# Attention scores: four 32-row groups of a batch issued together instead of two

## The reference, cut to what matters

```
x = x + attention(layernorm(x), ctx, ctx)          # layers 0 and 1
q, k, v = query @ Wq.T + bq, key @ Wk.T + bk, value @ Wv.T + bv    # 16 heads of 16
scores = einsum('bhsd,bhtd->bhst', q, k) / 4        # 128 x 128 for each batch and head
probs  = softmax(scores)                            # layer 1 adds a padding mask to the scores first
out    = einsum('bhst,bhtd->bhsd', probs, v) @ Wo.T + bo
```

## Time and profile before

| | |
|---|---|
| median of three runs | 1118.36 us |
| the profiled execution | 1119.13 us, its span 1117.3 us |
| PE busy | 952.8 us, 85% of the span |
| DVE busy | 776.6 us, 70% |
| ACT busy | 581.0 us, 52% |
| attention of layer 0 | about 49 to 232 us of the span |
| attention of layer 1 | about 600 to 768 us |
| score matmuls (L1343) | 512 records, 74.7 us of busy time in all |
| mean granted TensorE clock | 0.94 |

### The profile page before, as it was taken

The page is one execution under the profiler, slowest core; times in us unless marked ns, Lnnn a source line. Parts: engine busy times, 40 slices in busy tenths (PEclk is TensorE's granted clock), DMA queues, the critical chain, the costliest instruction groups (busy, mean ns, idle before and its releaser), DMA issues.

```text
span 1117.3 us, 20415 instructions
## 1 busy us (share of the span) xinstructions
PE 952.8 (85%) x6981; PEld 825.7 (74%) x6981; DVE 776.6 (70%) x1538; ACT 581.0 (52%) x1112; POOL 436.6 (39%) x479
## 2 busy tenths in 40 slices
PE   2798878748987999999837888885989999999995
PEld 2577667536877999999825767665678888888885
DVE  5688787866664777777655687795686666667665
ACT  5375675745234667667546877874622232322221
POOL 1465556240663666666415444334012212212210
PEclk9989999859998999999956899996899999999999
DMA  3300750010325888888540000001000001000002
GB/s 129 110 21 1 189 144 1 1 61 1 128 82 193 237 231 233 227 221 233 119 134 1 20 20 1 1 2 43 15 15 29 28 14 28 17 26 28 14 0 76
DMA packets 44281, 85.81 MB, mean 77 GB/s; under 512 B 4161, under 2 KB 31041, under 8 KB 44097
## 3 DMA queue, kind: packets, MB, share of 16 engines
q0 software_dynamic: 14784, 46.44, 15.1%
q1 hardware_dynamic: 29440, 38.61, 11.9%
HBM read 64.25 MB, written 20.79 MB: 76 GB/s over the span
## 4 chain that ended last, share of the span: by engine, by line
PE 48%; DVE 20%; ACT 11%; issue 9%; DMA 7%; POOL 4%; DVEq 0%; ACTq 0%; POOLq 0%
PE bank L1179 31%; PE bank L1215 8%; DMA w_raw<-in_fw,w_idx 4%; DVE nmax L1034 3%; PE bank L1274 3%; DVE probT_lo L1063 2%; PE bank L1364 2%; DVE prob L1037 2%; POOL sorted_x L375 2%; ACT xn L512 2%; DMA summed<-y_sb,tile_to 2%; ACT probT_hi L654 1%; ACT o_raw L644 1%; PE bank L1343 1%; ACT w_hi L533 1%
## 5 line engine op out<-in xcount | busy, mean ns | idle before, releaser
L1179 PE MATMUL bank<-xT_hi,w_hi 128*128 128x512 f32 x352 | 139.9, 398 | 2.2 <-DVE hid L964 2.2
L581 ACT ACTIVATE act_sb<-bank 128x512 f32<-128x512 f32 x88 | 52.6, 598 | 167.8 <-PE bank L1179 167.7
L1179 PE MATMUL bank<-xT_lo,w_hi 128*128 128x512 f32 x352 | 139.3, 396 | 0.0
L1179 PE MATMUL bank<-xT_hi,w_lo 128*128 128x512 f32 x352 | 139.1, 395 | 0.0
L964 DVE TENSOR_TENSOR hid<-bank,act_sb 128x512 f32<-128x512 f32 x88 | 60.8, 691 | 107.3 <-ACT act_sb L581 107.1
L332 POOL TENSOR_TENSOR w_hi<-w_raw,zero_col 128x768 fp32r<-128x768 f32 (+1 forms) x20 | 31.9, 1595 | 262.9 <-PE bank L1215 236.8
L951 DVE SCALAR_TENSOR_TENSOR xres<-bank,gate,xres 128x256 f32<-128x256 f32 x320 | 132.6, 476 | 0.8 <-PE bank L1215 0.8
L1364 PE MATMUL bank<-ident,prob 128*128 128x128 f32 x512 | 86.2, 298 | 31.9 <-DVE probT_lo L1063 26.0
L1063 DVE TENSOR_TENSOR probT_lo<-bank,probT_hi 128x512 f16<-128x512 f32 x128 | 88.0, 687 | 32.4 <-ACT probT_hi L654 31.8
L1179 PE MATMUL bank<-xsT_hi,w_hi 128*128 128x256 f32 x368 | 106.5, 289 | 2.3 <-DVE xsT_lo L918 1.5
L1215 PE MATMUL bank<-w_hi,hid_hi 128*128 128x256 f32 x352 | 99.5, 283 | 6.2 <-DVE hid_lo L972 6.2
(11 more groups left out here) (199 smaller groups left out, 2763.5 us busy)
## 6 DMA issues: line engine op xcount, KB each, us to landing
w_raw<-in_fw SPq DMA_DIRECT2D x18, 384.0 KB, 3.0
sorted_x<-empty_row SPq DMA_DIRECT2D x2, 2967.0 KB, 21.4
xs<-sorted_x SPq DMA_DIRECT2D x23, 258.0 KB, 3.4
ctx_raw<-in_ctxT SPq DMA_DIRECT2D x8, 512.0 KB, 5.2
aw_raw<-in_aw SPq DMA_DIRECT2D x10, 256.0 KB, 3.8
summed<-empty_row SPq DMA_DIRECT2D x1, 2304.0 KB, 29.6
xres<-in_x SPq DMA_DIRECT2D x4, 512.0 KB, 5.7
xn_all<-summed SPq DMA_DIRECT2D x4, 512.0 KB, 5.9
```

Source lines behind the costliest of these rows:

```text
L581: nc.scalar.activation(act_sb[:, (ls * J + j) % 2, :], bank[2 * ((ls * J + j) % 2) + 1][:], ACT.Silu).then_inc(f["act"], 1)
L1179: last = nc.tensor.matmul(dst, lh, rh, start=(i == 0), stop=(i == len(pairs) - 1))
```

## The change

`scores` now issues all four groups of a batch in one call, the first half of each of the four strips, in layer 1 then their masks, then the second half. It is called at steps 0, 4 and 8 rather than at every even step from 0 to 10, and once rather than twice ahead of the next block. Ahead of a batch it waits for both `sub` and for all four exponentials of the batch before. The number of matmuls is the same.

```diff
-                    b, g = divmod(i, NG)
+                    b = i // NG
...
                     if b >= 1:
-                        pe.wait_ge(a["sub"], n * 8 + (i - NG) // 2 + 1)
-                        pe.wait_ge(a["exp"], n * GROUPS + (i + 1 - NG + 1))
+                        pe.wait_ge(a["sub"], n * 8 + 2 * b)
+                        pe.wait_ge(a["exp"], n * GROUPS + i)
...
                     for u in range(KT):
-                        for r in (g, g + 1):
+                        for r in range(NG):
...
-                            for r in (g, g + 1):
+                            for r in range(NG):
...
                         if i + NG < GROUPS:
-                            if i % 2 == 0:
+                            if i % NG == 0:
                                 scores(n, i + NG)
...
                     if build:
-                        for g in range(0, NG, 2):
-                            scores(n + 1, g)
+                        scores(n + 1, 0)
...
-                for g in range(0, NG, 2):
-                    scores(0, g)
+                scores(0, 0)
```

## The result

The changed kernel takes 1174.51 us in the median (1172.32 to 1175.47, four runs), the kernel before beside it 1119.69 (four runs). The ratio is 1.048, with a 95% interval of 1.0449 to 1.0512: slower by 54.8 us, where 1172 had been predicted. The profiled execution of the changed kernel took 1175.47 us, with a span of 1173.6, which is 56.3 more than the span before.

A forecast was written before the change was run, and what follows sets the result against it. Though PE is busiest at 85%, a ring of ACT and DVE was taken to bound the edited steps. Waits of 37.9 us plus a clock term of 15.1 make 53.0 on 1119.13: 1172 us, range 1140 to 1194.

The forecast's parts named there:

- The saved calls count nothing: Score calls on PE: 29.8 us of work saved, counted at nothing because scores come 1.66 us early.
- the ring: Attention steps: ACT and DVE links E, O, H, L, M, sub, without PE; 3.66 us for two groups.
- The rival at 1089 us: Whole kernel: PE is the bound and the saved calls come back as time, 29.8 us; chance 0.06.
- The wait of 1.40, 1.44 and 1.62 us: Layer 0, steps 0, 4, 8: calls wait for the fourth exponential; 4.46 us a block, 37.9 us over both layers.
- The clock: Steps 4 and 8, three blocks per layer: PE's idle time halves its clock; 1.15 or 1.36 us each, 15.1 us.
- The clock's cost in the first blocks: First block of each layer: no clock cost counted, since the clock is at half there already.
- their terms: Last block of each layer, wait plus two slow calls: 6.76 us in layer 0, 7.7 us in layer 1.
- the column's sum: Predicted extra time of all eight blocks: each block's wait, plus two slow calls in all but the first blocks.
- That the time stays: Attention steps: engines emptying PSUM bound them, so saving and new wait both hide; 1119 us; chance 0.05.
- The waits without the clock: Attention: the waits cost 37.9 us and the clock holds, 1157 us; chance 0.27.
- The last rival: Attention: clock stays low through most, 1195 us, or strips don't run side by side, over 1180; chance 0.13.
- The beat between the calls of steps 4 and 8: Sign for the forecast: a batch takes 8.9 us or more instead of 7.3.

The follow-up runs named there:

- the first fill: Changed kernel with 14 unread matmuls on PE ahead of each wait of a later batch's score call: 1170.79 us, ratio 1.0452.
- the second fill: Changed kernel with seven unread matmuls ahead of T at steps 2, 3, 6 and 7, nine ahead of the calls of steps 4 and 8: 1167.64 us.
- the later copy: Kernel before, with ACT's output copy O moved from the end of an even step to behind H of the next odd step: 1113.17 us, ratio 0.9941.
- the first experiment: Kernel before, two groups to a call, only the first pair of each batch waiting for all four exponentials of the batch before: 1190.75 us, ratio 1.0639.

## Why the prediction was right

**The saved calls count nothing.** Right for steady steps. Doubled scores cost 0.9 us a block in layer 0, all of it at step 0, and O off the ring, with PE's work left as it was, shortened the beat by just its link. The rival at 1089 us is refuted: PE stood idle ahead of its score calls for 71.7 us, and no time was saved. The saving itself, worked out at 29.8 us, measured 18.7 on the score matmuls and 4.8 on the masks (17.8 to 13.0), as many calls ran at half the clock.

**The wait of 1.40, 1.44 and 1.62 us.** Measured without the clock in a block of layer 0: 1.34, 1.43 and 1.54, together 4.3 against 4.46. In layer 1 I had 1.59 for step 0, 1.63 for step 4 and 1.79 for step 8. In the changed kernel's third block there M(4), at full clock, is 8.85 us behind the block's start against 7.28, 1.57 late. Step 4 can be read in the second block with the first fill, whose clock was 1.00 from the block's start at 675.98 to E(8). E(8), first before (block from 644.85), then with the fill, with the call ahead of it:

```profile
660.40 0.65 ACT L632 ACTIVATE prob<-prob 128x512 f32<-128x512 f32 x1
```

```profile
691.95 0.71 PE L1348 MATMUL bank<-k_half,q_full 32*128 32x256 f32 x8
...
694.78 0.63 ACT L632 ACTIVATE prob<-prob 128x512 f32<-128x512 f32 x1 [0.25 <-DVE prob L1037]
```

The call starts 0.15 us after E(7) ends (691.80), and E(8) is 18.80 us behind the block's start instead of 15.55. That is 3.25 late, of which step 0 gave 1.56 and step 4 gives 1.69. For step 8, with the second fill, 740.55 (E(8)) to 748.26 (M(12)) is 7.71 us against 5.94, 1.77 late. Together 5.0 us, as predicted. That the ring takes over at its old beat after each stop, and PE is then ahead, held as well.

**The clock.** All calls at steps 4 and 8 of later blocks ran at half the clock for all or part of their time, behind 2.3 to 3.1 us of idle PE, as predicted. That it takes an idle time as long as these isn't borne out: with T and W moved into it, 0.35 to 1.01 us were left ahead of these calls, and eleven of the twelve were slow all the same. Its size comes out when the waits of 4.3 and 5.0 us are taken off the blocks. The four middle blocks leave 2.2, 1.9, 2.6 and 2.2 us, 8.9 in all, where 10.0 were predicted; in each third block one call was slow only in part. (The 0.2 us that the prediction adds for H are worked out from no row; they lie within these sums.) For the last blocks of the two layers it isn't separated, so of the 15.1 us a part stays argued. The second fill gave only 6.9 us back in the medians (1174.51 - 1167.64). But it also cost something: the calls at step 0, which it doesn't fill, ran slower than in the changed kernel in four of the six later blocks (1.65 to 2.18 us against 1.15 and 1.37), and in the first blocks its own matmuls ran at a low clock (seven took 1.86 us instead of 1.09) and held up T.

**What was off.** Two things. The clock's cost in the first blocks was put at nothing, as it is at half there already. In layer 0 the first block cost 6.16 us instead of 4.46: its three calls all run at 2.09 us, while before the clock rose within the block. With the first fill 2.6 us of that come back, and 2.2 in layer 1's first block. So that layer 1's first block came to 5.07 us against 5.0 is luck: M(4), E(8) and M(12) are 1.92, 2.48 and 4.87 us late there, steps of 1.92, 0.56 and 2.39 and not three of 1.6 to 1.8. And in the last block of a layer ACT has no next context to split, so nothing covers part of the wait at step 4: at full clock, with the first fill, it costs 1.9 us in layer 0 and 2.1 in layer 1, not 1.44 and 1.63. Up to the end of the attention the last blocks cost 8.4 and 8.8 us, 1.7 and 1.1 above their terms; the rest of these two differences isn't traced. The three misses, 4.4 us, less the 1.3 by which the other blocks fell short in sum, make the 3.1 us between the column's sum and the 56.0 us of the attention.

**The rivals.** That the time stays fell by the first run. The Trainium skill, page TensorEngine Tiling (Array Packing), section PSUM Bottleneck, has packing speed up TensorE and not the emptying of PSUM; the trace agrees on that (18.7 us of PE work saved, no time gained). What the packing did here is to hold the next scores until the last bank is read. The waits without the clock, 1157 us, were the nearest rival; the fill at 1167.64 with a clean block of 50.30 against 52.24 us decides against it. The last rival falls too: the strips run side by side in the new order (1.15 us a call, 1.37 with masks), and the clock was back at full at step 0 of every later block but one. The beat between the calls of steps 4 and 8 in layer 0, expected at 8.9 us or more, is 10.00 with a low clock and 8.93 to 8.94 without.

## What to carry over

Before work is merged into larger calls, ask what each small call waited for: the merged one waits for the last of them all, and all engines behind it wait too. Work saved on the engine with the highest busy share is worth little where a ring of other engines sets the beat; follow one beat through the timelines, and shorten a link of that ring, as the later copy did. And idle time bought on PE is paid twice, since the clock can fall in it.

## What the runs showed of the hardware

- Score matmuls on two or four strips take nearly the same time at either clock: 8 records 1.13 us and 16 records 1.15 at full, 2.08 and 2.09 at half. That fits the first experiment, whose pairs at half clock cost a batch two calls of 2.08.
- The clock fell without a long idle time too. With T moved ahead of the call no idle time of PE from 111 to 128 us was above 1.65 us, and still T went from 0.66 us to 1.09 and the call from 1.15 to 2.09. With unread matmuls in those stretches (the last experiment) it held at 1.00 for a block of 50.30 us.
- A fill that comes after the fall costs what it should save: the same 14 matmuls took 1.94 us at full and 3.36 at half clock, and the call behind them started 1.37 us after its exponential instead of 0.14.
